# Zero products added to the dense accumulator of a two-layer token tower

## What is computed

```python
h = tok(x)                       # rows of a table of 4360
h = h + L0_attn(ln(h))           # gated Toeplitz convolution, done by FFT
h = h + L0_ffn(ln(h))            # product-key memory and causal attention, 8 heads
h = h + L1_attn(ln(h))           # softmax attention, one head
h = h + L1_ffn(ln(h))            # 8 experts, top 2, behind a residual of its own
```

```python
scores, idx = top_k(sim, 16)     # twice, for the two halves of a key
final, pk = top_k(scores[0][..., :, None] + scores[1][..., None, :], 16)
k = einsum('bnhk,bnhkd->bnhd', softmax(final), keys_table[ind])
v = einsum('bnhk,bnhkd->bnhd', softmax(final), values_table[ind])
```

## Time and profile before

| | |
|---|---|
| time, median of 3 runs | 3515.86 us (3515.56 to 3523.73) |
| span of the profiled execution | 4054.8 us |
| TensorE matmul busy | 3145.7 us, 78% |
| VectorE busy | 2896.5 us, 71% |
| ScalarE, GpSimd busy | 2063.6 us, 2009.3 us |
| mean granted TensorE clock | 0.865 |

### The profile page before, as it was taken

How to read it: one execution, slowest core, us unless ns; L and a number is a source line. 1 busy time by engine, 2 the same in 40 slices (tenths; PEclk the granted TensorE clock), 3 DMA queues, 4 the chain that set the end, 5 groups by cost and what they waited for, 6 DMA issues and landing times.

```text
span 4054.8 us, 40659 instructions
## 1 busy us (share of the span) xinstructions
PE 3145.7 (78%) x9980; PEld 1450.3 (36%) x9980; DVE 2896.5 (71%) x9977; ACT 2063.6 (51%) x4521; POOL 2009.3 (50%) x2084
## 2 busy tenths in 40 slices
PE   4895165687878787988887777889786778787898
PEld 2452022243434242433343333334343333333434
DVE  5435877778787777787788787877878787864423
ACT  3112145555555555555557565556585646555422
POOL 3000166666666665555555565565555565655200
PEclk9997577897989897988989888989888989888887
DMA  0121012121212121212121211111111212111000
GB/s 13 40 70 29 28 45 65 42 63 43 63 43 64 42 62 40 62 41 59 38 57 44 56 51 52 49 53 50 50 49 46 58 47 56 46 55 41 21 3 3
DMA packets 87160, 186.50 MB, mean 46 GB/s; under 512 B 40231, under 2 KB 42188, under 8 KB 86926
## 3 DMA queue, kind: packets, MB, share of 16 engines
q0 software_dynamic: 66560, 135.40, 12.7%
q1 hardware_dynamic: 20366, 48.53, 3.8%
HBM read 182.74 MB, written 1.05 MB: 45 GB/s over the span
## 4 chain that ended last, share of the span: by engine, by line
DVE 38%; PE 25%; issue 10%; another core or an unknown queue 9%; ACT 7%; DVEq 0%; ACTq 0%
DVE mx_W L1455 8%; PE mx_acc L1098 6%; PE mx_O L1110 5%; DVE mx_KVs L1623 4%; PE mx_area L1144 3%; ACT mx_GT L1360 3%; DVE mx_mx_part L1643 2%; PE mx_D L1088 2%; ACT mx_W L1292 2%; DVE mx_hot L1589 1%; DVE mx_mx L1643 1%; DVE mx_hot L1588 1%; DVE mx_S L1473 1%; DVE mx_row L1591 1%
## 5 line engine op out<-in xcount | busy, mean ns | idle before, releaser
L1070 POOL DMA_INDIRECT mx_G<-in_kv_table,mx_slot_i x2048 | 1977.6, 966 | 1781.5 <-DVE mx_W L1455 646.6
L1098 PE MATMUL mx_acc<-mx_W,mx_table 128*128 128x512 f32 x2048 | 1198.4, 669 | 0.4 <-ACT mx_kvT L1299 0.4
L1455 DVE SCALAR_TENSOR_TENSOR mx_W<-mx_D,mx_W 128x512 f32<-128x512 f32 x1024 | 704.2, 688 | 482.2 <-remote 221.3
L1292 ACT ACTIVATE mx_W<-mx_D 128x512 f32<-128x512 f32 x1024 | 607.0, 593 | 528.9 <-PE mx_D L1088 251.2
L1360 ACT ACTIVATE mx_GT<-mx_G,mx_slot_w 128x128 f32<-128x128 f32 x2048 | 758.5, 494 | 17.7 <-DVE mx_KVs L1623 13.4
L1088 PE MATMUL mx_D<-mx_U,mx_pick_b 96*128 96x512 bf16 x1024 | 437.7, 427 | 163.1 <-DVE mx_W L1455 127.3
L1098 PEld LDWEIGHTS mx_acc<-mx_W,mx_table 128*128 128x128 f32 x2048 | 443.0, 218 | 197.9 <-issue 119.5
L1316 ACT ACTIVATE mx_PT<-mx_area 128x512 f32<-128x512 f32 x480 | 247.5, 516 | 456.0 <-PE mx_area L1148 120.8
L1110 PE MATMUL mx_O<-mx_PT,mx_KVs 128*65 128x512 f32 (+3 forms) x768 | 333.7, 518 | 106.8 <-ACT mx_OT L1308 72.5
L1124 PE MATMUL mx_area<-mx_KTa,mx_QTa 64*128 64x512 f32 (+3 forms) x384 | 207.4, 625 | 229.0 <-DVE mx_mx_part L1643 138.2
L1623 DVE TENSOR_REDUCE mx_KVs<-mx_GT 128x128 f32<-128x2048 f32 x128 | 291.8, 2280 | 7.3 <-ACT mx_GT L1360 6.6
(11 more groups left out here) (350 smaller groups left out, 4604.3 us busy)
## 6 DMA issues: line engine op xcount, KB each, us to landing
mx_table<-in_kv_dense SPq DMA_DIRECT2D x64, 512.0 KB
mx_G<-in_kv_table,mx_slot_i POOLq DMA_INDIRECT x2048
cv_table<-in_c_idft SPq DMA_DIRECT2D x12, 512.0 KB, 3.2
cv_table<-in_c_dft SPq DMA_DIRECT2D x6, 512.0 KB, 3.3
cv_table<-in_c_idft SPq DMA_DIRECT2D x4, 256.0 KB, 3.2
out_h<-mx_xc SPq DMA_DIRECT2D x4, 256.0 KB
mx_G<-in_c_pick SPq DMA_DIRECT2D x1, 528.0 KB
st_h<-in_tok_W,em_ids POOLq DMA_INDIRECT x32
```

What stands on the lines that cost most here:

```text
L1070: pool.indirect_dma_start(G[g % RING][:, r, :], None, a["kv_table"], bass.IndirectOffsetOnAxis(slot_i[n % 2][:, k, r:r + 1], 0))\
L1098: pe.matmul(acc[:, :], table[:, tile, :], W[c % TILE_RING][:, :], start=(tile == 0), stop=(tile == TILES - 1)).then_inc(applied, 1)
L1292: act.activation(W[c % TILE_RING][:, :], D_ps[c % 3][:, :], ACT.Exp).then_inc(p_done, 1)
L1455: dve.scalar_tensor_tensor(W[c % TILE_RING][:, :], D_ps[c % 3][:, :], 0.0, W[c % TILE_RING][:, :], ALU.is_ge, ALU.mult).then_inc(w_done, 1)
```

## The change

At the end of each position of the dense loop, unless the tile is the last of its half, TensorE adds up to four products of zero weights to `acc`. `streamed(cnt, q)` counts the columns that the position streams by its plan (four per float32 column, one per bfloat16 column; the two areas of `fill_scores`, which use 64 of the array's rows each, count once), and `(4800 - streamed) // 512` products fill up to 4800. Their stationary operand is a zero column of `mask_b`, repeated 128 times (96 rows x 128 columns, bfloat16), the moving operand 512 columns of `pick_b`. They neither start nor stop the accumulation, wait for no semaphore and signal none. What `acc` holds is not changed.

```diff
+STEADY = 4800
...
+def streamed(cnt, q):
+
+
+    c = q - SLOT
+    total = 0
+    if 0 <= c + 3 < PAIRS * SLOT:
+        total += HALF * (2 if corner_of(tile_of(c + 3)[2])[3] else 1)
+    if 0 <= c < PAIRS * SLOT:
+        total += 4 * HALF
+    for use in area_uses(q - 2):
+        if use in cnt.weigh:
+            total += 4 * (HALF - piece(use)[2])
+    for use in area_uses(q)[:1]:
+        kind, _, _, r = use
+        if kind == "S":
+            total += 4 * ((r + 1) * P if r < 4 else HALF if r % 2 == 0 else ((r - 4) // 2 + 1) * P)
+        elif kind == "ST":
+            total += 4 * (HALF - piece(use)[2])
+        else:
+            total += 4 * HALF
+    key = cnt.x_at.get(divmod(q, SLOT))
+    if key is not None:
+        total += {"U": 8 * P, "post": 4 * P, "KK": 4 * P, "l1x": 4 * P, "l2x": 4 * P, "l2r": 4 * NB * E,
+                  "Y": 16 * (D + 1), "l1y": 16 * (D + 1)}.get(key[0], 4 * HALF)
+    return total
...
+            def add_zeros(count):
+                zeros = mask_b[0:96, 0, 0:1].broadcast_to([96, P])
+                flat = pick_b[:, :, :].rearrange("p a c -> p (a c)")
+                for _ in range(count):
+                    pe.matmul(acc[:, :], zeros, flat[:, 0:HALF], start=False, stop=False, skip_group_check=True)
...
                 if 0 <= c < PAIRS * SLOT and late:
                     apply_dense(c)
+                if 0 <= c < PAIRS * SLOT and c % TILES != TILES - 1:
+                    add_zeros(max(0, STEADY - streamed(cnt, q)) // HALF)
```

## The result

The change makes the kernel slower: 3542.23 us (3535.08 to 3547.89) against 3516.99 us, ratio 1.0067, 95% interval 1.0054 to 1.0080. Forecast were 3504 us, between 3455 and 3560, and 0.45 for faster. The time lies in the range, on the other side.

The account below looks back on a forecast made before the run. No engine full; VectorE has 38% of the chain, TensorE 25%, with 26% of the loop at 1.2 GHz. Price 38 less clock gain 54 gives -16 us, taken as some 12: 3515.9 - 12 = 3504 us, range 3455 to 3560.

Parts of the forecast that it names:

- the clock's term: Dense loop: products lift TensorE's clock; gain between 0 and 108 us, half of the bound taken, 54 us.
- I take 20% of 189 = 38 us: Price of the 851 products outside slot 1, by TensorE's share of the chain in first halves; bounds 0 and 189 us.
- Slot 1 at nothing: Slot 1: 209 products, 46.5 us, cost nothing, as TensorE idles 75 us and the chain is VectorE's and the gathers'.
- The signs: Loop clock 0.93 or more, slot 1 above 0.9, first halves 0.9, shorter maxima waits, L1098 towards 600 ns, few new-line pieces.
- The one with a chance of 0.22: After second halves and at p 35 to 41, products stand in TensorE's path: +36 us, 3552 us; chance 0.22.
- The fourth rival: In the loop, products of 96 rows and zero weights do not lift the clock: 3541 us; chance 0.07.
- Full recovery (0.12): Clock recovers nearly everywhere, denser work also ending dips of following stretches: 70 us gained, 3446 us; chance 0.12.
- Both terms end in idle time: VectorE and the gathers set the pace, so nothing measurable: 3516 us; chance 0.19.

Follow-up runs that it names:

- the ordinary profile: The kernel before, no edit, profiled once more: span 3517.3 us, timed ratio 1.0004 to the kernel before.
- one and the same kernel: Three products ahead of each fill_scores at p 16 to 30 of slots 2 to 16, none at position ends, against the kernel before: 1.0033, again 1.0018.

## Why the prediction was wrong

**The profile it rested on.** I noted that its span was 538.9 us above the timed runs and took its proportions all the same. They were wrong where it mattered: low clock 26% of the loop (14% in an ordinary execution), TensorE 25% of the chain (38%), idle time of TensorE in a first half 29 of 103 us (19 of 83). The guess that VectorE's instructions would be shorter in timed runs is refuted: they last as long, and the waits are gone.

**The step that failed** is the clock's term, "I take half of the bound, 54 us". The bound, 108 us, was TensorE's 25% of the chain times the 26% at low clock, halved: both shares from the long execution, and the low clock spread evenly over TensorE's part of the chain. In the ordinary profile TensorE's pieces of the loop's chain that ran at 1.2 GHz add up to 106 us (3 + 71 + 12 + 20 in the table above), in the runs with products in slot 1 alone and at p of 32 and above alone to 66 and 68 us. Full clock would take off half of that, 33 to 53 us. So the 54 us were all that there was to win, not half of it, and the change doesn't get it all. It takes away 148 us of low clock, but 42 of them in slot 1 and 61 at p 16 to 31, where the gathers and VectorE set the pace and TensorE has only 3 + 12 us of low clock on the chain, worth 8 us at most. At p below 16 it takes away 45 us, worth 23 us at most; at p of 32 and above, where TensorE leads, none. By this estimate the clock gave back some 30 us at most, in place of 54.

**The price.** "I take 20% of 189 = 38 us" can't be called wrong or right. The change costs 24 us, which is the price less 0 to 30 us given back, so the price is 24 to 54 us, 13% to 29% of the 189. Measured with the clock unchanged are the products at p of 32 and above: 9 of 38 us, and doubled 33 of 77 us, 43%. With 38 us of price and 30 us given back at most the sum is above zero already: the small clock term alone turns the forecast's sign. The 81 us of the new line on the chain are no measure of the price, since 9 of them lie in slot 1 (5.9% of its 156 us) and cost nothing.

**Slot 1 at nothing** was right, for a reason I had only half seen: the gathers pace it.

**The signs.** Nearly all signs that I had named for being right came: the loop's clock at 0.96, slot 1's at 0.93, the first halves' at 0.96, the apply product's mean at 615 ns (from 633 ns in the ordinary profile and not from 669), shorter waits for the maxima, a new line with 2.3% of the chain. They tell that the clock rose. They could not tell whether the time that it rose in was on the path.

**The rivals.** The one with a chance of 0.22, slower with the products in TensorE's path, is what happened, at 3542 us where it said 3552. Its place was right: 18 of 22 us at p of 32 and above, 5 us at p below 16; its 40% uncovered and 40 us given back are not shown. The fourth rival's 3541 us is nearest to the measured time by luck: it had the clock stay, and the clock rose. Full recovery (0.12) falls, since even 128 rows do not reach it. "Both terms end in idle time" holds for slot 1, and for slot 16 in the sum.

**The skill's rule.** By the Trainium skill (TensorE: Matmul & The Clock Gate, Part 1), activity releases the throttle. The trace agrees in the direction, 0.93 to 0.96 in the loop. That it isn't the time alone for which the engine is busy is shown in slot 1, which lasts as long with 32 rows as with 96: TensorE is busy for 151.54 of 157 us with 32 rows and for 138.09 of 156 us with 96, and its clock is the lower one, 0.90 against 0.93.

```profile
480.00:637.00 157.00, 151.54 (x470) 53.03 (x469) 137.97 (x533) 94.52 (x216) 117.78 (x122) 0.90 0.24 62
```

**Still open:** what the long waits of the first profile were, how the 24 us divide into price and clock more closely than above, how much of the loss with 32 rows is the clock's, and why the 336 to 360 products ahead of the areas lengthen the positions behind them.

## What to carry to other kernels

Filling an engine's idle time to hold its clock pays only if the low clock is on the chain: here 14% of the loop was at 1.2 GHz, but mostly in the halves that VectorE paces and in slot 1, while part of the 1060 x 0.2225 us went where TensorE leads. So ask first how much of the engine's own chain runs at low clock; half of that is all that can be won. Before building on a profile, hold its span beside the timed runs; if they differ by more than the spread of the runs, take another. And of a filling that costs X and gives back Y, try to measure both, but check in the trace that the control really costs the same: the one tried here, 32 rows, took 0.19 us more per dose and lifted the clock as well, so it split nothing.

## What the runs showed of the hardware

- An execution of the same program can be 15% longer mostly by waits (4054.8 against 3517.3 us): VectorE's mask lasts 688 ns in both, a gather's issue 966 and 972 ns. Only TensorE is slower, by its clock (the apply product 669 against 633 ns).
- Products of zero weights lift the granted clock: 0.914 to 0.935 with 96 or 128 rows. With 32 rows the profiled run has 0.923, over a longer run, while TensorE is busy for 3220 us against 3110.
- Behind a float32 product on 128 rows, a dose of bfloat16 products on 32 rows starts 0.10 us later than one on 96, and the 96-row product behind it again 0.10 us later (0.96 against 0.86 us, twice). Between products of one dose there is no difference.
- Repeated on another chip, one and the same kernel gave 1.0033 and 1.0018 to before, each interval 0.0026 or less wide.
